# Dense groups of a four-layer graph network: each engine's operations spread over the four slots of a group, and three operations on other engines

## The reference

```
x1 = norm(x + x@Ws + bs)                              # layer 1 without messages
h2 = relu(x1@W1 + b1) @ W2                            # layer 2, HID = 256
x2 = norm(x1 + h2 + b2)
x3 = norm(x2)                                         # layer 3 without messages
h  = relu(x3@root1 + b1r)
out = norm(x3 + h@root2 + b2r)                        # layer 4
```

## Time and profile before

| | |
|---|---|
| median of 3 runs | 2678.92 us (2676.92 to 2681.65) |
| profiled execution | 2694.78 us, span 2693.0 us |
| TensorE busy | 2202.6 us (82%) |
| VectorE busy | 2105.2 us (78%) |
| GpSimd busy | 1565.0 us (58%) |
| ScalarE busy | 1469.3 us (55%) |
| mean granted TensorE clock | 0.924 of full speed |

### The profile page before, as it was taken

The page is one execution under the profiler, slowest core; times in us unless marked ns, Lnnn a source line. Parts: engine busy times, 40 slices in busy tenths (PEclk is TensorE's granted clock), DMA queues, the critical chain, the costliest instruction groups (busy, mean ns, idle before and its releaser), DMA issues. The chain is left out here.

```text
span 2693.0 us, 53316 instructions
## 1 busy us (share of the span) xinstructions
PE 2202.6 (82%) x12829; PEld 1706.9 (63%) x12829; DVE 2105.2 (78%) x7193; ACT 1469.3 (55%) x4919; POOL 1565.0 (58%) x1653
## 2 busy tenths in 40 slices
PE   2998888888667776998776998567679999899996
PEld 2886667667555555886664898456646666555553
DVE  3667998899757776886897786588868888688886
ACT  0575555556556665665444777388844444333332
POOL 2778888888444435664886876333334444255554
PEclk9999999999878787999998989688889999899998
DMA  4666666666533435554675554344332223211221
GB/s 87 215 220 210 208 203 202 209 203 207 144 130 129 134 115 156 170 166 142 203 218 174 165 172 154 108 126 135 123 120 80 80 81 85 69 48 55 57 58 31
DMA packets 291561, 376.34 MB, mean 140 GB/s; under 512 B 59002, under 2 KB 142896, under 8 KB 291258
## 3 DMA queue, kind: packets, MB, share of 16 engines
q1 hardware_dynamic: 265658, 321.84, 37.6%
q0 software_dynamic: 25600, 51.09, 7.4%
HBM read 167.38 MB, written 206.80 MB: 139 GB/s over the span
## 5 line engine op out<-in xcount | busy, mean ns | idle before, releaser
L1808 PE MATMUL phase_p_w<-phase_w_rel,phase_rowsT 128*128 128x512 f32 (+1 forms) x1200 | 511.1, 528 | 10.3 <-ACT phase_rowsT L1861 10.2
L1889 DVE SCALAR_TENSOR_TENSOR phase_added<-phase_p_w,relation,phase_added 128x128 f32<-128x128 f32 x1200 | 349.9, 340 | 22.9 <-PE phase_p_w L1808 21.2
L1084 PE MATMUL phase_p_sum<-phase_whole,phase_link 128*128 128x128 f32 (+2 forms) x792 | 199.6, 338 | 146.7 <-ACT phase_whole L1201 65.3
L324 ACT ACTIVATE phase_sq<-phase_y 128x512 f32<-128x512 f32 x294 | 186.2, 634 | 229.9 <-POOL phase_y L457 178.9
L773 POOL DMA_INDIRECT phase_rows<-X,src_row x200 | 191.4, 957 | 202.0 <-PE phase_p_T L1816 168.0
L384 PE MATMUL phase_p_h<-W2c,phase_g 128*128 128x128 f32 x1568 | 231.5, 310 | 86.6 <-DVE phase_h L439 71.9
L384 PEld LDWEIGHTS phase_p_h<-W2c,phase_g 128*128 128x128 f32 x1568 | 220.3, 224 | 93.7 <-issue 77.1
L773 POOL DMA_INDIRECT phase_rows<-H,src_row x200 | 192.7, 963 | 135.0 <-PE phase_p_T L1816 108.8
L1152 POOL TENSOR_TENSOR phase_message<-R,scores 128x128 f32<-128x128 f32 x200 | 92.6, 464 | 284.3 <-PE phase_p_sum L1084 282.0
L1084 PEld LDWEIGHTS phase_p_sum<-phase_whole,phase_link 128*128 128x128 f32 x792 | 135.1, 213 | 188.2 <-ACT phase_whole L1201 87.8
L1808 PEld LDWEIGHTS phase_p_w<-phase_w_rel,phase_rowsT 128*128 128x128 f32 x1200 | 189.6, 193 | 86.6 <-issue 41.1
(11 more groups left out here) (254 smaller groups left out, 6876.6 us busy)
## 6 DMA issues: line engine op xcount, KB each, us to landing
H<-phase_h SPq DMA_DIRECT2D x196, 256.0 KB, 2.8
X<-phase_x SPq DMA_DIRECT2D x196, 256.0 KB, 2.3
phase_same<-same_keys SPq DMA_DIRECT2D x175, 256.0 KB
phase_xT<-in_x_columns SPq DMA_DIRECT2D x98, 256.0 KB, 4.0
Z<-phase_x SPq DMA_DIRECT2D x98, 256.0 KB
phase_x<-X SPq DMA_DIRECT2D x98, 256.0 KB
out<-phase_o SPq DMA_DIRECT2D x98, 256.0 KB
H<-R SPq DMA_DIRECT2D x50, 256.0 KB, 2.4
```

The costliest lines, as they stand in the source:

```text
L324: act.activation(self.buf(dst, g)[:, :, :], self.buf(src, g)[:, :, :], ACT.Square).then_inc(self.S[dst], 1)
L1084: last = nc.tensor.matmul(p[:, 0:width], loads.link(t), whole[1 - v][:, 0:width], start=False, stop=True)
L1808: nc.tensor.matmul(p_w[(PARTS * (t % UNROLL) + n) % BANKS][:, 0:b - a, :], rowsT[v][:, :], w[:, a:b, :], start=True, stop=True).then_inc(s ...
L1889: nc.vector.scalar_tensor_tensor(out=added[v][r % 2][:, :], in0=p_w[(PARTS * (t % UNROLL) + n) % BANKS][:, r % RG, :], scalar=plane(D["rel ...
```

## The change

Three operations of the second layer go to other engines: the copy of h2 from PSUM from VectorE to ScalarE, y2 = h2 + x1b from GpSimd (reading the copy) to VectorE (reading PSUM, after the copy), and x3 from VectorE to GpSimd. g0 and g1 are issued apart, and x2 is split into two halves that count four times on its semaphore (`PARTS`). TensorE's next h2 now waits for y2 and not for the copy.

Offsets after, in FirstLayers: ScalarE x2's halves 37 (1) and 38 (2), two roots 33 (1), square 31 (3), copy of h2 28 (0), g1 25 (1), g0 22 (2), x1T 20 (0), root 14 (2), square 11 (3). VectorE two inverses 34 (2), sum 32 (0), y2 29 (1), inverse 15 (3), sum 13 (1), y1 10 (2). GpSimd x3 37 (1), x1b 26 (2), x1 16 (0). TensorE h2 26 (2), g1 24 (0), g0 21 (1), x1T 19 (3), y1 8 (0). x1T and g0 get a second buffer, h2 one fewer. The class has 430 slots for 435, so D gets 76.

In LastLayers the same operations stay on their engines; hT goes to slot 11 on TensorE and 12 on ScalarE, y4 to 13 and 14, square to 18, sum to 19, root to 20, inverse to 21, o to 22, x3b from 8 to 12. The class has 413 slots for 409, so I gets 74.

```diff
     def made(self, eng, n, g, back=0):
-        wait(eng, self.S[n], g + 1 - back)
+        wait(eng, self.S[n], self.PARTS.get(n, 1) * (g + 1 - back))
...
-    SLOTS = 4 * (GROUPS - 1) + 47
+    SLOTS = 4 * (GROUPS - 1) + 42
+    PARTS = {"x2": 4}
...
-        if (g := self.group(s, 30)) is not None:
+        if (g := self.group(s, 26)) is not None:
             self.made(pe, "g0", g)
             self.made(pe, "g1", g)
-            self.made(pe, "h2", g, 1)
+            self.made(pe, "y2", g, 1)
...
-        if (g := self.group(s, 26)) is not None:
-            self.made(pe, "x1T", g)
-            for k in range(2):
+        for k, offset in ((1, 24), (0, 21)):
+            if (g := self.group(s, offset)) is not None:
+                self.made(pe, "x1T", g)
...
     def act(self, act, s):
-        if (g := self.group(s, 44)) is not None:
...
+        for half, offset in ((1, 38), (0, 37)):
+            if (g := self.group(s, offset)) is not None:
+                self.made(act, "r2", g)
+                self.made(act, "y2", g)
+                self.left_by_store(act, "x2", g)
+                for t in (2 * half, 2 * half + 1):
+                    act.activation(self.buf("x2", g)[:, t, :], self.buf("y2", g)[:, t, :], ACT.Copy, scale=self.buf("r2", g)[:, t:t + 1]).then_inc(self.S["x2"], 1)
...
         if (g := self.group(s, 28)) is not None:
-            for k in range(2):
+            self.left_by_store(act, "h2", g)
+            self.made(act, "p_h2", g)
+            act.copy(self.buf("h2", g)[:, :, :], self.P["p_h2"][:, :, :]).then_inc(self.S["h2"], 1)
+        for k, offset in ((1, 25), (0, 22)):
+            if (g := self.group(s, offset)) is not None:
                 self.read_out_relu(act, f"g{k}", f"p_g{k}", "p_h2", g, self.W["b_W1"][:, k:k + 1])
...
     def dve(self, dve, s):
-        if (g := self.group(s, 44)) is not None:
-            self.made(dve, "r3", g)
-            self.left_by_store(dve, "x3", g)
-            self.nc.vector.tensor_tensor(self.buf("x3", g)[:, :, :], self.buf("y2", g)[:, :, :], over_rows(self.buf("r3", g)), ALU.mult).then_inc(self.S["x3"], 1)
...
-            self.nc.vector.tensor_copy(self.buf("h2", g)[:, :, :], self.P["p_h2"][:, :, :]).then_inc(self.S["h2"], 1)
+            self.nc.vector.tensor_tensor(self.buf("y2", g)[:, :, :], self.P["p_h2"][:, :, :], self.buf("x1b", g)[:, :, :], ALU.add).then_inc(self.S["y2"], 1)
...
     def pool(self, pool, s):
-            pool.tensor_tensor(self.buf("y2", g)[:, :, :], self.buf("h2", g)[:, :, :], self.buf("x1b", g)[:, :, :], ALU.add).then_inc(self.S["y2"], 1)
...
+            pool.tensor_tensor(self.buf("x3", g)[:, :, :], self.buf("y2", g)[:, :, :], over_rows(self.buf("r3", g)), ALU.mult).then_inc(self.S["x3"], 1)
...
-    SLOTS = 4 * (GROUPS - 1) + 21
+    SLOTS = 4 * (GROUPS - 1) + 25
```

More of the change, by code:

```diff
@@ L392, in pe @@
                                       start=True, stop=True).then_inc(self.S[f"p_g{k}"], 1)
-        if (g := self.group(s, 22)) is not None:
+        if (g := self.group(s, 19)) is not None:
             self.made(pe, "x1", g)
@@ L432, in dve @@
             self.inverse(dve, "r3", "sd3", "x3", g)
[L433 removed]
+        if (g := self.group(s, 32)) is not None:
             self.total(dve, "ss2", "sq2", ("sd2", "sd3"), g)
[L435 removed]
+        if (g := self.group(s, 29)) is not None:
             self.made(dve, "p_h2", g)
[L437 to L439 removed]
@@ L440, in dve @@
-        if (g := self.group(s, 18)) is not None:
+            self.made(dve, "h2", g)
+            self.made(dve, "x1b", g)
+            self.left(dve, "y2", "sq2", g)
+            self.left(dve, "y2", "x2", g)
+            self.left(dve, "y2", "x3", g)
+            self.nc.vector.tensor_tensor(self.buf("y2", g)[:, :, :], self.P["p_h2"][:, :, :], self.buf("x1b", g)[:, :, :], ALU.add).then_inc(self.S["y2"], 1)
+        if (g := self.group(s, 15)) is not None:
             self.inverse(dve, "r1", "sd1", "x1", g)
-        if (g := self.group(s, 14)) is not None:
+        if (g := self.group(s, 13)) is not None:
@@ L450, in pool @@
     def pool(self, pool, s):
[L451 to L456, removed]
-            pool.tensor_tensor(self.buf("y2", g)[:, :, :], self.buf("h2", g)[:, :, :], self.buf("x1b", g)[:, :, :], ALU.add).then_inc(self.S["y2"], 1)
-        if (g := self.group(s, 22)) is not None:
+        if (g := self.group(s, 37)) is not None:
+            self.made(pool, "r3", g)
+            self.made(pool, "y2", g)
+            self.left_by_store(pool, "x3", g)
+            pool.tensor_tensor(self.buf("x3", g)[:, :, :], self.buf("y2", g)[:, :, :], over_rows(self.buf("r3", g)), ALU.mult).then_inc(self.S["x3"], 1)
+        if (g := self.group(s, 26)) is not None:
             self.made(pool, "x1", g)
@@ L461, in pool @@
             pool.tensor_tensor(self.buf("x1b", g)[:, :, :], self.buf("x1", g)[:, :, :], over_tiles(self.W["b2c"]), ALU.add).then_inc(self.S["x1b"], 1)
-        if (g := self.group(s, 20)) is not None:
+        if (g := self.group(s, 16)) is not None:
             self.made(pool, "r1", g)
@@ L484, in sp @@
             sp.dma_start(self.buf("x3", g)[:, :, :], rows(self.io["X3"], g)).then_inc(self.loaded[g % RING], 16)
-        if (g := self.group(s, 20)) is not None:
+        if (g := self.group(s, 24)) is not None:
             self.store(sp, "o", g)
@@ L494, in pe @@
             self.transposes("p_h", "hT", g)
-        if (g := self.group(s, 12)) is not None:
+        if (g := self.group(s, 13)) is not None:
             self.made(pe, "hT", g)
             self.products("p_y4", "hT", "root2c", g)
-        if (g := self.group(s, 10)) is not None:
+        if (g := self.group(s, 11)) is not None:
             self.made(pe, "x3T", g)
@@ L507, in act @@
     def act(self, act, s):
-        if (g := self.group(s, 16)) is not None:
+        if (g := self.group(s, 20)) is not None:
             self.root(act, "sd4", "ss4", "r4", g, "eps", 1.0 / F)
-        if (g := self.group(s, 14)) is not None:
+        if (g := self.group(s, 18)) is not None:
             self.square(act, "sq4", "y4", "ss4", g)
@@ L515, in act @@
             act.copy(self.buf("h", g)[:, :, :], self.P["p_h"][:, :, :]).then_inc(self.S["h"], 1)
-        if (g := self.group(s, 11)) is not None:
+        if (g := self.group(s, 12)) is not None:
             self.read_out_relu(act, "hT", "p_hT", "p_h", g, self.W["b_root1"][:, :])
@@ L533, in pool @@
     def pool(self, pool, s):
-        if (g := self.group(s, 18)) is not None:
+        if (g := self.group(s, 22)) is not None:
             self.made(pool, "r4", g)
@@ L537, in pool @@
             pool.tensor_tensor(self.buf("o", g)[:, :, :], self.buf("y4", g)[:, :, :], over_rows(self.buf("r4", g)), ALU.mult).then_inc(self.S["o"], 1)
-        if (g := self.group(s, 8)) is not None:
+        if (g := self.group(s, 12)) is not None:
             pool.wait_ge(self.loaded[g % RING], 16 * (g // RING + 1))
```

33 lines of the change are left out of this document (14 added, 19 removed), and 2 rows, old and new, of tables (PARTS, SLOTS).

## The result

| | before | after |
|---|---|---|
| median of the runs | 2679.0 us (2676.92 to 2681.65, 4 runs) | 2559.59 us (2555.44 to 2561.95, 4 runs) |
| profiled span | 2693.0 us | 2558.4 us |
| mean granted TensorE clock | 0.924 | 0.944 |

The ratio is 0.9552, 95% interval 0.9536 to 0.9569. The forecast was 2617 (2580 to 2662).

What follows compares the result with a forecast made beforehand. GpSimd's queue was taken to bound B, and in D a serial carry behind one ScalarE and one TensorE burst per group. Terms +3 - 21 - 4 - 40 - 2 + 2 = -62 gave a 2617 us median, range 2580 to 2662.

Steps and rivals of the forecast that it cites:

- the sum of -62: Whole kernel: A +3, B -21, C -4, D -40, E and G -2, I +2 us.
- The first sum: Stage B: x3 for y2 on GpSimd -0.23, x1b shorter -0.26 us a group, over 54.5 groups -27 us.
- a bound of -32: Stage B's far end: -32 us if the gather behind x1b also falls to the length of the others.
- VectorE still has its product (twice a group) and the comparison of keys: Stage B: these VectorE operations read two SBUF tensors, so -21 us was taken instead of -27.
- The account of ScalarE's four slots: Stage D: ScalarE's 4.39 us burst plus a 0.5 us copy, spread into steps of 2.0, 2.6, 2.4 and 2.1 us.
- A bare step: Stage D: a step without dense work, priced at 1.1 us, with 34 of them in the 99 intervals.
- so I leave some waits in: Stage D: operations on different engines now meet one or two slots apart, so -40 was taken from -59 to -43 us.
- I carry the difference over unchanged: Whole kernel: the median lies 15.9 us below the profiled execution, and was assumed to do so after the change too.
- (1): Stage B: TensorE's next h2 waits for y2 through a longer relay, +125 us, 2764 in all; chance 0.10 with milder forms.
- (2): B gains but D does not, through TensorE's low clock or other waits: -22 us, about 2657; chance 0.17.
- (3): GpSimd still delayed by the lock and the bursts otherwise covered: -4 us and less, no change; chance 0.04.
- (4): More gain: B -32, D -59, with C and a higher clock, about -95 us, 2584; chance 0.11.

Runs made afterwards that it cites:

- e3: Kernel before with only the three operations on their new engines, at the old offsets, y2 in the slot of TensorE's next h2: 2694.44 us.
- e2: Kernel after with LastLayers as before, so only FirstLayers is changed: 2563.07 us.
- e11: Kernel after with x3 back on VectorE and LastLayers as before: 2522.70 us.
- e9: e3 with y2 on VectorE one slot earlier, 33 for 34, a slot ahead of TensorE's next h2: 2645.44 us.
- e12: Kernel after with y2 one slot later, 30 for 29, in the slot of TensorE's next h2: 2600.23 us.
- e5: Kernel after with x3 back on VectorE, at its new offset: 2515.74 us.
- e7: Kernel after with ScalarE's FirstLayers operations, all but one root, again in one slot of four, dependent ones later: 2629.09 us.
- e6: Kernel after with x1b on VectorE instead of GpSimd, in the same slot: 2537.41 us.
- e8: Kernel after with TensorE's x1T, g0, g1 and h2 again in one slot of the four: 2624.09 us.
- e1: Kernel before, unchanged, run again for a second profile: 2676.89 us.
- e4: Kernel after with the three operations back on their old engines, in slots near the new ones: 2619.03 us.

## Why the prediction was wrong

Against the second profile of before the sum of -62 should have been -116.5. The mechanisms of B and D were the right ones; two terms of the sum were too small and carry 49 of the 54.5 us. E to H add 12 more, and I takes 7 back.

**B, predicted -21, measured -41.** The first sum was -27 from two prices, x3 for y2 and x1b back to its length of A; these were right to 0.01 us (0.23 and 0.25). What failed first is what it left out: the two xs gathers (0.19 us a group, about 10 us; I had allowed it for one, as a bound of -32) and the gaps (0.14, about 7). The second failing step is "VectorE still has its product (twice a group) and the comparison of keys", by which -27 became -21. The product did meet GpSimd's operations, and VectorE took all of it, 1597 ns for 332. e3 bears out that this is free: GpSimd's group is 8.12 us there too (402.57 to 410.69), with the product at 411 ns. The Trainium skill (SBUF — State Buffer, "two separate sides") has the loser of the ports fully blocked, and the product's row agrees. Here the loser was VectorE, for which B doesn't wait.

**D, predicted -40, measured -69.** The account of ScalarE's four slots held almost to the digit: in the timeline the starts from one x2 half to the next `whole` are 1.53 and 1.35 us (I had 1.55 and 1.35). What was too dear was the rest of a step. Slots came out at 1.83, 2.44, 2.18 and 1.85 us, 8.3 together, where I had 9.5 to 10.5: g1 and y1 on TensorE do not stand in front of the carry as I priced them (1.83 for 2.35), and h2 runs at the high level (1.95 us), which removes the upper end of 3.4. A bare step was priced too low, 1.1 us for a measured 1.4, which gives 10 us back. By the measured numbers 16.2 x 8.3 + 34 x 1.4 = 182 us, which is the 99 intervals of 1.84. The other failing step is the last one: -59 to -43 was worked out and -40 taken, "so I leave some waits in". ScalarE's waits before `whole`, for deg and for the sum, are 9.3 us between 725 and 905, and they are in the 1.84 already. The clock's gain (0.80 to 0.93) stood in the sum only as h2's two prices; what it is worth by itself no run separates.

**E to H, predicted -2, measured -13.6.** The spread of LastLayers was priced at -2 because "TensorE is already at 92% of E"; by e2 it brings 12.4 in E, F and H, 7.5 of them in E itself, so the 8% was not out of reach. The rest is within what two profiles differ by.

**I, predicted +2, measured +8.6.** The two more table loads are there (36 for 35 at the exponentials, 15 for 14 at the roots, 1283 ns each), 2.6 us. e2 and e11 show that the rise belongs to LastLayers' new slots: without them I is 250.0. The other 6 us may come with the one further group that I now holds, whose TensorE and VectorE work I didn't price; that is not shown.

**A, C, J and K.** +3.8 for +3, -6.1 for -4, 0.8 for 0. A's agreement is partly luck: e2 holds the same operations in A and is 1.0 above before.

**The profile's own time.** "I carry the difference over unchanged" did no harm to the forecast of the median, since both were lowered by 15.9, but for the wrong reason: 9.3 of the 15.9 were G's stretch at the low level in that execution.

**The rivals.** (1) did not happen in B: TensorE waited 0.5 us in all for y2 between 240 and 645, and in e3, where it waited 52.0 us in B, B still gained. It is real where I did not look for it, in D, when y2 shares h2's slot: 38 us of D between e3 and e9, 32 between e12 and after. I had put its price on the lengths of the relay; what decides is the order of the queues within one slot. (2) and (3) are out. (4), at -95 and 2584, was nearest, for its reasons, B and D at their far ends; both went beyond them (-41 for -32, -69 for -59), and E to H gave 13.6 for 2. Caution was taken off in B and in D in the same direction, 6 us and some 11, but that is only part of the miss: without it the forecast would have been about 2600, still 40 above the time.

**x3's new engine.** The Trainium skill (GPSIMD Engine Reference, Engine selection) warns of twice the time; the trace has 1045 ns on GpSimd for 681 to 695 alone on VectorE, 1.5 times. As a price that was answered correctly. As a direction the rule was right: e5 shows that x3's move costs 44 us, because GpSimd sets B's pace. I compared x3 on GpSimd only with y2 on GpSimd, and never with GpSimd having neither.

## What to carry to other kernels

Where a serial carry passes between two in-order queues, price each step as the longer of the two queues between hand-overs; work bunched on either engine costs its whole length once per period, and a producer is best put a slot ahead of its consumer, not in the same one: one slot was worth 32 to 38 us of D here. When an operation is shown too long because two engines hold each other up, find out which one sets the pace, and what of the other engine it falls beside; a slot where it meets no such operation cures it, and the operation itself (x3) may be best left where it is. A bound is only as wide as the terms in it: here both far ends together gave 2584, and what no term held, the second gather, the gaps and TensorE's cheaper steps, lay beyond.

## What the runs showed of the hardware

TensorE can stay at its lower level for a long time while it is full. In the profiled run of e7, stage G from 1480 us on (same columns as above):

```profile
1480.00:1490.00 10.00, 10.00 (x84) 9.06 (x82) 9.16 (x35) 8.50 (x42) 8.60 (x9) 1.00 0.65 214
1490.00:1500.00 10.00, 8.37 (x46) 7.76 (x46) 7.36 (x28) 5.41 (x28) 8.58 (x9) 0.69 0.51 165
1500.00:1520.00 20.00, 20.00 (x87) 18.24 (x87) 7.17 (x29) 9.37 (x44) 9.35 (x10) 0.50 0.24 77
1520.00:1600.00 80.00, 80.00 (x346) 73.16 (x345) 35.17 (x140) 37.22 (x174) 36.84 (x36) 0.50 0.31 100
1600.00:1640.00 40.00, 40.00 (x174) 36.58 (x173) 17.20 (x74) 18.43 (x89) 17.44 (x18) 0.50 0.33 106
1640.00:1660.00 20.00, 20.00 (x171) 18.95 (x170) 16.47 (x62) 16.52 (x81) 16.49 (x17) 0.99 0.55 180
```

Ahead of it TensorE was busy 8.37 of 10 us; then the granted clock is 0.50 (1.2 GHz) for 140 us in which the engine is never idle, and it comes back with the engine still full. This costs 67 us of G, and it is not a property of e7: its other four runs are 2627 to 2629, 71 us below the profiled 2700. In e5 it lasts from 1380 to 1440, after a stretch of 8.63 busy of 10, and 20 us in the first profile of before; e6, e8 and e12 have it in G too (222 to 233 us), e1 to e4 and e9 to e11 don't in theirs. What makes it begin in one execution and not in the next, and what ends it, stays open. A profile whose time is off its median should be searched for such a stretch before anything is reasoned from it.
